# Two layers of modulated attention on one core: the keys' rotation moved in GpSimd's order, and layer 1's causal mask of the maxima moved from TensorE to DVE

## What is computed

```
h = layernorm(x) * (1 + ca) + sa
x = x + ga * attention(h)
h = layernorm(x) * (1 + cb) + sb
x = x + gb * feed_forward(h)
```

```
q, k = apply_rope(q), apply_rope(k)
scores = einsum('bhqd,bhkd->bhqk', q, k) / sqrt(head_dim)
scores = where(tril, scores, very_negative)
out = softmax(scores) @ v
```

## Time and profile before

| | |
|---|---|
| Median of 3 runs | 1895.84 us (1892.85 to 1897.75) |
| The profiled execution | 1891.85 us, its span 1890.1 us |
| TensorE busy | 1730.7 us, 92% of the span, 9031 matmuls |
| DVE busy | 1156.7 us, 61% |
| ScalarE busy | 809.6 us, 43% |
| GpSimd busy | 885.1 us, 47% |
| Mean granted clock of TensorE | 0.97 of 2.4 GHz |
| DMA | 63.38 MB, 34 GB/s |

### The profile page before, as it was taken

One profiled execution on the slowest core, in us unless ns is written; L12 is line 12 of the kernel. 1 busy time (PEld: TensorE's weight loads), 2 busy tenths in 40 slices (PEclk: granted clock), 3 DMA queues, 4 the chain that ended last, 5 costly groups with the idle time before them and its releaser, 6 DMA issues. The chain is left out here.

```text
span 1890.1 us, 25001 instructions
## 1 busy us (share of the span) xinstructions
PE 1730.7 (92%) x9031; PEld 1264.5 (67%) x9031; DVE 1156.7 (61%) x2249; ACT 809.6 (43%) x1780; POOL 885.1 (47%) x784
## 2 busy tenths in 40 slices
PE   5699999999999999999999599998859999999778
PEld 3567777777777776777777388876735555555457
DVE  6856666566666575656655833345787666664475
ACT  3445454545445454545454221100315566566221
POOL 1686786876867868678774400000351222210200
PEclk9899999999999999999999899999879999999989
DMA  5101101010110110100100312102200000000021
GB/s 185 34 28 35 34 18 45 18 45 18 34 37 26 30 33 17 40 28 23 34 12 1 114 52 66 30 1 97 81 1 1 1 1 1 1 1 1 28 44 45
DMA packets 75315, 63.38 MB, mean 34 GB/s; under 512 B 23470, under 2 KB 53358, under 8 KB 75194
## 3 DMA queue, kind: packets, MB, share of 16 engines
q1 hardware_dynamic: 75194, 61.79, 11.0%
HBM read 59.68 MB, written 2.10 MB: 33 GB/s over the span
## 5 line engine op out<-in xcount | busy, mean ns | idle before, releaser
L844 ACT ACTIVATE a_probs<-psum,a_neg_max 128x128 f32<-128x128 f32 (+7 forms) x256 | 190.2, 743 | 265.3 <-DVE a_neg_max L768 265.0
L768 DVE CUSTOM_DVE_ANT_0 psum<-psum,a_keys_allowed 128x128 f32<-128x128 f32 (+7 forms) x256 | 195.4, 764 | 133.9 <-PE psum L77 133.7
L698 PE MATMUL psum<-a_probsT,a_v 128*128 128x512 f32 (+3 forms) x768 | 258.4, 486 | 0.2 <-ACT a_probsT L855 0.2
L1649 DVE TENSOR_REDUCE a_neg_max<-psum 128x1 f32<-128x512 f32 (+3 forms) x384 | 194.8, 553 | 97.2 <-PE psum L1569 62.6
L698 PEld LDWEIGHTS psum<-a_probsT,a_v 128*128 128x128 f32 x768 | 144.7, 190 | 117.3 <-issue 91.8
L1712 ACT ACTIVATE a_probsT<-psum 128x512 f32<-128x512 f32 (+3 forms) x384 | 173.3, 495 | 93.7 <-PE psum L1550 69.5
L780 DVE SCALAR_TENSOR_TENSOR x<-psum,a_row_inv,x 128x512 f32<-128x512 f32 x256 | 191.2, 749 | 16.9 <-PE psum L77 10.6
L785 DVE TENSOR_TENSOR a_ctxT_lo<-psum,a_ctxT_hi 128x512 fp32r<-128x512 f32 x64 | 44.3, 692 | 215.9 <-ACT a_ctxT_hi L861 215.9
L855 ACT COPY a_probsT<-psum 128x512 f32<-128x512 f32 (+3 forms) x384 | 171.0, 484 | 9.9 <-PE psum L685 9.8
L685 PE MATMUL psum<-ident,a_probs 128*128 128x128 f32 x1152 | 171.7, 274 | 0.4 <-ACT a_probsT L855 0.4
L75 PE MATMUL psum<-a_kT_hi,a_qT_lo 128*128 128x512 f32 (+3 forms) x384 | 150.6, 392 | 21.1 <-POOL a_qT_lo L567 21.1
(11 more groups left out here) (300 smaller groups left out, 4071.8 us busy)
## 6 DMA issues: line engine op xcount, KB each, us to landing
a_raw_q<-in_L_attn_qw_q SPq DMA_DIRECT2D x32, 256.0 KB, 4.0
a_raw_o<-in_L_attn_qw_o SPq DMA_DIRECT2D x32, 256.0 KB, 2.7
a_raw_scale_o<-in_L_attn_scales_o SPq DMA_DIRECT2D x32, 256.0 KB, 3.7
mod1b_w<-in_L_wmod SPq DMA_DIRECT2D x4, 1024.0 KB, 11.4
mod0a_w<-in_L_wmod SPq DMA_DIRECT2D x3, 1024.0 KB, 10.4
mod0b_w<-in_L_wmod SPq DMA_DIRECT2D x3, 1024.0 KB, 7.3
f_raw<-in_L_ffn_down_w SPq DMA_DIRECT2D x10, 256.0 KB, 3.1
f_raw<-in_L_ffn_gate_w SPq DMA_DIRECT2D x10, 256.0 KB, 3.3
```

The lines of the kernel that those rows point to most:

```text
L698: last = nc.tensor.matmul(bank(use)[:, first:HALF], v[:, g % 2, j, :], probsT[b][:, j, first:HALF], start=(j == 0), stop=(j == keys - 1))
L768: nc.vector.tensor_tensor_reduce(out=scores, in0=scores, in1=keys_allowed[:, S - (i + 1) * P:S], scale=-1.0, scalar=-MASKED, op0=ALU.add, ...
L844: nc.scalar.activation(probs[:, u % 3, 0:(i + 1) * P], score[u % 2][:, 0:(i + 1) * P], ACT.Exp, bias=neg_max[:, h % 2, i:i + 1], scale=-1. ...
L1649: nc.vector.reduce_max(neg_max[:, c, i, h:h + 1], y_bank[n % SLOTS][:, 0:keys], AX.X, negate=True).then_inc(maxed.sem, 1)
```

## The change

Two edits that have nothing to do with each other.

The first is in layer 0's attention. The halves of the next group's keys are rotated in heads 1 and 2 of a group and no longer in heads 0 and 1, in the list of names and in the loop alike. When the keys' projections are made, by whom, and where the rotated keys are read stays the same.

The second is in layer 1's attention. The mask matmul of the y pieces is gone. DVE's maximum of a piece with the diagonal becomes the instruction of layer 0, with a mask of its own, `allowed`, of 512 columns; pieces without a diagonal keep the reduction. GpSimd fills and draws `allowed` in the opening, and DVE waits for it (`cleared` at 7) before its first step.

```diff
-        if h % REP0 < 2 and h // REP0 < LAST_GROUP:
-            pool_ropes.append(("k", h // REP0 + 1, h % REP0))
+        if h % REP0 in (1, 2) and h // REP0 < LAST_GROUP:
+            pool_ropes.append(("k", h // REP0 + 1, h % REP0 - 1))
...
-                if h % REP0 < 2 and h // REP0 < LAST_GROUP:
-                    turn(("k", h // REP0 + 1, h % REP0))
+                if h % REP0 in (1, 2) and h // REP0 < LAST_GROUP:
+                    turn(("k", h // REP0 + 1, h % REP0 - 1))
...
+        allowed = sb("allowed", [P, HALF])
...
-            for buffer in (zero[:, :], k_stack[:, :, :, :]):
+            for buffer in (allowed[:, :], zero[:, :], k_stack[:, :, :, :]):
...
             stack_q((0, 0), 0)
+            pool.affine_select(out=allowed[:, HALF - P:HALF], in_=allowed[:, HALF - P:HALF], compare_op=ALU.is_ge,
+                               fill=MASKED, base=0, pattern=[[-1, P]], channel_multiplier=1).then_inc(cleared, 1)
             stack_q((0, 0), 1)
...
-                diagonal = c == b
-                out = y_bank[n % SLOTS]
-                last = nc.tensor.matmul(out[:, 0:keys], qA[:, h // 2, tile(i)],
-                                        kA[:, h % 2, c * HALF:c * HALF + keys], start=True, stop=not diagonal)
-                if diagonal:
-                    last = nc.tensor.matmul(out[:, keys - P:keys], mem.ident_bf[:, :], mem.causal[:, :],
-                                            start=False, stop=True)
-                last.then_inc(y_scored.sem, 1)
+                nc.tensor.matmul(y_bank[n % SLOTS][:, 0:keys], qA[:, h // 2, tile(i)],
+                                 kA[:, h % 2, c * HALF:c * HALF + keys], start=True, stop=True).then_inc(y_scored.sem, 1)
...
-                nc.vector.reduce_max(neg_max[:, c, i, h:h + 1], y_bank[n % SLOTS][:, 0:keys], AX.X,
-                                     negate=True).then_inc(maxed.sem, 1)
+                scores, neg = y_bank[n % SLOTS][:, 0:keys], neg_max[:, c, i, h:h + 1]
+                if c == i // TPH:
+                    nc.vector.tensor_tensor_reduce(out=scores, in0=scores, in1=allowed[:, HALF - keys:HALF], scale=-1.0,
+                                                   scalar=-MASKED, op0=ALU.add, op1=ALU.min, accum_out=neg
+                                                   ).then_inc(maxed.sem, 1)
+                else:
+                    nc.vector.reduce_max(neg, scores, AX.X, negate=True).then_inc(maxed.sem, 1)
...
+            dve.wait_ge(cleared, 7)
             turn((0, -1), (0, 0), order_first)
```

More of the change, by code:

```diff
@@ L1435, in _ @@
                 counter.open(pool)
-            pool.wait_ge(cleared, 2)
+            pool.wait_ge(cleared, 3)
             def from_group(group, width):
@@ L1490, in _ @@
                 pool.memset(buffer, 0.0).then_inc(cleared, 1)
-            pool.wait_ge(cleared, 4)
+            pool.wait_ge(cleared, 5)
             pool.memset(v[:, :, HD1:HD1 + 1], 1.0).then_inc(cleared, 1)
-            pool.wait_ge(cleared, 5)
+            pool.wait_ge(cleared, 6)
             stack_q((0, 0), 0)
+            pool.affine_select(out=allowed[:, HALF - P:HALF], in_=allowed[:, HALF - P:HALF], compare_op=ALU.is_ge,
+                               fill=MASKED, base=0, pattern=[[-1, P]], channel_multiplier=1).then_inc(cleared, 1)
             stack_q((0, 0), 1)
```

## The result

| | before | after |
|---|---|---|
| Median | 1895.83 us (1892.85 to 1897.75) | 1862.38 us (1861.12 to 1863.17) |
| Ratio, 95% interval | | 0.9824 [0.9807, 0.9841] |
| Span of the profiled execution | 1890.1 us | 1860.4 us |
| Mean granted clock | 0.97 | 0.96 |

The kernel is 33.45 us faster; 35.5 were predicted. Behind this agreement errors of opposite sign are hidden, and the profile shows them.

The account below looks back on a forecast made before the run. TensorE was taken to bound layer 0's attention and layer 1's turns, DVE the opening. Keys 19, turns 16 and opening 0.5 summed to 35.5 us off the median 1895.84, giving 1860.3, range 1851 to 1871.

Parts of the forecast that it names:

- The keys, mechanism: Layer 0's attention: rotating keys one head later ends the queries' second half in time, margin 2.9 us in second and third heads.
- The keys, size: Layer 0's attention: moving the keys' rotation one head later gains 19 us, range 18 to 21.
- a stall of 1.47 us costs 1.3 us; the rest is caught up: Layer 0's attention: heads with TensorE's stall for GpSimd's rotation take 31.48 us, those without 30.19; 14 stalls give 18.2 us.
- The mask's price on TensorE: Layer 1's turns: a mask costs 0.12 us before a score (17 of 32), 0.07 elsewhere (15); 3.1 us a turn.
- I let these eat a quarter: Layer 1's turns: three places near DVE or ScalarE leave 2.3 of 3.1 us a turn, 16 us for seven.
- The places that I named: Layer 1's turns: last maxima with normalization behind, keys' copy from the stage bank behind three maxima, bursts of five maxima.
- nothing gained: End of a layer 1 turn: two masks at the last maxima, with the normalization behind them, save no time.
- The opening: Start of layer 1's attention, bound by DVE: 32 fewer masks gain 0.5 us, range -1 to +1.5.
- Rival 1: Layer 1: accumulator reads in a row take their 0.14 us and maxima set the pace; gain 23, 1873 us, chance 0.12.
- Rival 3: Layer 1's opening: TensorE's clock falls with less work, first microseconds of turns at half speed; 3 to 4 us, 1864, chance 0.08.
- Rivals 4 and 5: Layer 0 keys still delay queries' second half, 1879, chance 0.04; layer 1 maxima don't overlap, 1914, chance 0.03.
- Rival 2: Both layers: everything comes through, whole stalls and 3.1 us per turn; gain 44.5, 1851 us, chance 0.12.

## Why the prediction was right, and where it was not

**The keys, mechanism: right.** GpSimd's order after, in the third head of a group, whose two halves and keys stand in one row. The timeline of GpSimd, first operation of the queries' first half, of the keys, of the second half, and its last:

```profile
348.57 1.29 POOL L558 TENSOR_TENSOR a_turned_pool<-a_q_sum,a_sine 64x512 f32<-64x512 f32 x1 [2.82 <-DVE a_q_sum L754]
...
356.49 1.28 POOL L558 TENSOR_TENSOR a_turned_pool<-a_k_sum,a_sine 64x512 f32<-64x512 f32 x1
...
364.43 1.28 POOL L558 TENSOR_TENSOR a_turned_pool<-a_q_sum,a_sine 64x512 f32<-64x512 f32 x1
...
370.93 1.27 POOL L567 TENSOR_TENSOR a_qT_lo<-a_q_sum,a_qT_hi 128x512 fp32r<-128x512 f32 x1
...
378.33 1.28 POOL L558 TENSOR_TENSOR a_turned_pool<-a_q_sum,a_sine 64x512 f32<-64x512 f32 x1 [0.81 <-DVE a_q_sum L754]
```

Keys without a wait ahead of them, the second half done at 372.20, wanted at about 374.8 (14.4 us behind the head's first maximum, as before): a margin of 2.6, where 2.9 was worked out. The output weights hide, with 0.81 us to spare.

**The keys, size: 25.1 instead of 19, above the term's range.** The step that failed is "a stall of 1.47 us costs 1.3 us; the rest is caught up". The 1.3 was the difference of two heads, 31.48 and 30.19, and the second is not the first without its stall: it carries about 0.43 us more, as long as its transposes of values. The right comparison gives 1.74, and nearly all of it is a stall's loss from start to start, of which the idle time in the record is only a part. The timeline of TensorE before, whose next row is the 352.52 of the earlier trace rows, and the same place after:

```profile
350.67 0.38 PE L685 MATMUL psum<-ident,a_probs 128*128 128x128 f32 x2
...
344.70 0.38 PE L685 MATMUL psum<-ident,a_probs 128*128 128x128 f32 x2
344.84 0.47 PE L75 MATMUL psum<-a_kT_hi,a_qT_lo 128*128 128x512 f32 x1
```

From the transposes to the product it took 1.85 us and takes 0.14: 1.71 are lost, not 1.47. My "at most 14 stalls in full, 21.1" had the same error, and was no bound. 14 x 1.74 = 24.4, and the first stall makes the rest: the same two instructions stood 2.36 us apart there.

**The mask's price on TensorE: right at its places.** The timeline of TensorE after, at the place of the earlier trace rows: from the y piece to the x piece behind it 1592.98 - 1592.86 = 0.12 us, before 1618.89 - 1618.73 = 0.16; and that x piece lasts 0.23 to the next start instead of 0.31. So 0.04 + 0.08 = 0.12, as worked out. The 0.07 taken for the 15 other places wasn't measured one by one, and with it the 3.1 us of a turn stay an estimate.

```profile
1592.86 0.28 PE L1567 MATMUL psum<-hT_lo,hT_hi 128*128 128x256 f32 x1
1592.98 0.40 PE L1550 MATMUL psum<-hT_hi,hT_lo 128*128 128x512 f32 x1
1593.21 0.39 PE L1567 MATMUL psum<-hT_lo,hT_hi 128*128 128x512 f32 x1
```

**How much of it arrives: 1.54 per turn, not 2.3.** The step that failed is "I let these eat a quarter": of the estimated 3.1 us they ate half. The places that I named are those where a loss shows, and the first half of the rows is where more of it is: 16 masks gave 0.46 us there, against 1.09 in the second half. I had the burden of the first half of a turn as an average (205 of 305 us) and not as what it is, seven maxima in succession behind a copy of 1.39 us. At the boundary "nothing gained" was right: the stall is 0.15 us longer, and the last head's four masks just make up for it.

**The opening: -1.1, not +0.5,** just outside my bounds of -1 to +1.5. DVE's price was put at 0.5 us for 32 maxima and the clock's at nothing; together they are about 1.0 us more than with the masks on TensorE, and their shares weren't separated. What TensorE was to win there before 1405 doesn't show.

**The rivals.** Rival 1 (reads in a row) is right that they cost something, 0.02 to 0.05 us, at most a third of its price. The Trainium skill's rule ("VectorE: DVE Perf Modes", section "The DRAIN you can't avoid") does not show between these instructions: the next one starts 0.60 us after one that lasts 0.69. The same section of the Trainium skill adds that a next operation which is not held back starts earlier, and the prediction left that out; the 0.60 us fit the exception. Rival 3 (the clock) came true in part: in the opening, at a price that wasn't separated, and at a place it did not name, behind the boundaries, where a fall of 3.4 us cost a turn 0.9 to 1.6 us. Rivals 4 and 5 had no part in it. Rival 2 was true of the keys alone.

**The sum.** 19 + 16 + 0.5 = 35.5 was 25.1 + 9.5 - 1.1 = 33.5: turns 7 x 1.54 = 10.8, less one fall of 1.4, and 0.1 of the last turn. The forecast of 1860.3 was 2 us from the result because +6 and -8 cancelled, which is luck, not because its terms were good; by themselves the keys were above their range (25.1 in 18 to 21), the opening just below its own, and the turns low in theirs (9.5 in 8 to 22).

## What to carry to other kernels

Price a stall against the same unit of work without it: look for what else the units that don't stall do, and take start to start, not the idle time of the record (1.71 against 1.47 us here). A saving on the busiest engine arrives only where the next engine isn't already late, so read the bursts one by one; putting the instruction that the bound engine waits for ahead of bookkeeping of the same engine was worth 5.7 us of layer 1's attention here, where all the masks gave 8.4. And an experiment that moves a step must move it over the boundary that is measured.

## What the runs showed of the hardware that I had not expected

TensorE's granted clock fell to 1.2 GHz within 2.1 us of a single stall of 1.4 to 1.9 us, in stretches where it had been at 2.4 GHz and 37.64 of 38.00 us busy; a fall of 3.4 us cost a turn 0.9 to 1.6 us, in most cases 1.4 or more (the 0.9 in the kernels with the mask alone, 42.95, and with the first half on TensorE, 43.41 against 42.48), one of 6.8 us 2.7. Behind 18 stalls of 0.83 us there were none, behind six of 1.87 us four. A wait of 1.5 us can so cost another 0.9 to 2.7. Equal stalls with equal work around them brought a fall at one moment and none at another; what decides was not settled.

The product of 512 columns behind a mask of 128 columns in bfloat16 lasts 0.08 us longer from start to start, which is more than the mask's own 0.04. The type need not be the reason: in layer 0 a product of 512 columns behind one of 128, both f32 in the profile's rows, takes 0.29 us too (345.90 to 346.19 in the changed kernel), where behind one of 512 it takes 0.23. The maximum of 512 columns with a mask and its read of the accumulator take no longer than the plain reduction where the two alternate (0.60 and 0.61 us), and 0.02 to 0.05 us more where they follow each other.
